# An intermediate tile of the second feed-forward stage made as two products of 256 columns

## The reference

```python
h = _ln(x) * g2 + beta2
ff = _gelu2(h @ W1 + b1) @ W2 + b2
return x + ff
```

## Time and profile before

| what | value |
|---|---|
| median of 3 runs | 2416.95 us (2416.4 to 2420.13) |
| the profiled execution, its time | 2414.24 us |
| its span | 2412.5 us |
| granted TensorE clock, mean | 0.997 |
| TensorE matmul rows, busy | 2364.6 us (98%) |
| TensorE weight loads, busy | 1891.9 us (78%) |
| DVE, ACT, POOL busy | 1349.5, 1009.7, 1017.0 us |
| matmuls | 16068 |

### The profile page before, as it was taken

One profiled execution on the slowest core, in us unless ns is written; L12 is line 12 of the kernel. 1 busy time (PEld: TensorE's weight loads), 2 busy tenths in 40 slices (PEclk: granted clock), 3 DMA queues, 4 the chain that ended last, 5 costly groups with the idle time before them and its releaser, 6 DMA issues. The chain is left out here.

```text
span 2412.5 us, 42169 instructions
## 1 busy us (share of the span) xinstructions
PE 2364.6 (98%) x16068; PEld 1891.9 (78%) x16068; DVE 1349.5 (56%) x2749; ACT 1009.7 (42%) x2057; POOL 1017.0 (42%) x829
## 2 busy tenths in 40 slices
PE   8999999999999899999999999998999999999999
PEld 6788888888887677777777777766888888888887
DVE  7354454454556777777777777778443333323322
ACT  6132232231332776767667676767311111111111
POOL 0042242341424796767677676766112202202200
PEclk9999999999999999999999999999999999999999
DMA  7110111101123466565556566564320110110110
GB/s 229 45 44 18 43 37 41 43 17 61 43 96 115 128 192 198 160 212 162 195 162 205 168 194 191 173 190 168 129 70 1 52 52 0 52 52 5 47 35 18
DMA packets 142196, 243.92 MB, mean 101 GB/s; under 512 B 14140, under 2 KB 28620, under 8 KB 142048
## 3 DMA queue, kind: packets, MB, share of 16 engines
q1 hardware_dynamic: 142048, 241.92, 31.4%
HBM read 216.69 MB, written 25.20 MB: 100 GB/s over the span
## 5 line engine op out<-in xcount | busy, mean ns | idle before, releaser
L1218 POOL TENSOR_TENSOR at_bias<-at_bias,at_mask 128x512 f32<-128x512 f32 x512 | 591.8, 1185 | 234.4 <-DMA at_bias<-in_fside_Bx16xSxS 212.3
L645 ACT ACTIVATE L_hid<-bank,L_b1c 128x512 f32<-128x512 f32 x256 | 176.6, 690 | 963.4 <-PE bank L290 958.6
L837 DVE CAST L_hh<-L_hid 128x512 fp32r<-128x512 f32 x256 | 122.5, 478 | 748.5 <-PE bank L946 715.1
L288 PE MATMUL bank<-xth,L_w1h 128*128 128x512 f32 x1024 | 402.9, 393 | 1.4 <-DVE xtl L730 1.4
L944 PE MATMUL bank<-L_w2h,L_hh 128*128 128x512 f32 x1024 | 401.1, 392 | 0.0
L289 PE MATMUL bank<-xth,L_w1l 128*128 128x512 f32 x1024 | 399.4, 390 | 0.0
L290 PE MATMUL bank<-xtl,L_w1h 128*128 128x512 f32 x1024 | 399.2, 390 | 0.0
L946 PE MATMUL bank<-L_w2l,L_hh 128*128 128x512 f32 x1024 | 398.7, 389 | 0.0
L945 PE MATMUL bank<-L_w2h,L_hl 128*128 128x512 f32 x1024 | 398.5, 389 | 0.0
L1274 ACT ACTIVATE at_bias<-at_bias,cos_sin 128x512 f32<-128x512 f32 x512 | 363.2, 713 | 9.1 <-DVE cos_sin L1412 9.1
L1412 DVE CUSTOM_DVE_ANT_0 at_bias<-bank,at_bias 128x512 f32<-128x512 f32 x512 | 331.7, 683 | 36.7 <-PE bank L1595 24.0
(11 more groups left out here) (205 smaller groups left out, 3211.4 us busy)
## 6 DMA issues: line engine op xcount, KB each, us to landing
at_bias<-in_fside_Bx16xSxS SPq DMA_DIRECT2D x256, 512.0 KB, 3.7
L_ring<-in_L_cond_w SPq DMA_DIRECT2D x32, 256.0 KB, 4.6
L_xres<-in_x SPq DMA_DIRECT2D x8, 1024.0 KB, 5.3
x_scratch<-L_xres SPq DMA_DIRECT2D x8, 1024.0 KB, 4.3
at_xres<-x_scratch SPq DMA_DIRECT2D x32, 256.0 KB, 4.3
L_xin<-x_scratch SPq DMA_DIRECT2D x8, 1024.0 KB, 5.6
L_xres<-x_scratch SPq DMA_DIRECT2D x8, 1024.0 KB, 5.5
L_xin<-in_x SPq DMA_DIRECT2D x7, 1024.0 KB, 5.3
```

Source lines behind the costliest of these rows:

```text
L288: nc_mm = pe.matmul(out, ah, bh, start=i == 0, stop=False)
L645: nc.scalar.activation(hid[m % 2][:, :], turn[m % 2][:, :], func, bias=b1c[:, m:m + 1]).then_inc(h_act, 1)
L1218: nc.gpsimd.tensor_tensor(tile, tile, mask[:, m % TT, :], ALU.add).then_inc(masked, 1)
```

## The change

For the second feed-forward stage alone, `up` calls `split_product` twice for each intermediate tile: first for columns 0 to 255 of the moving operand and of the bank, then for columns 256 to 511. Each call has its own 12 matmuls with their 12 weight loads, the same 12 weight blocks in both. The waits stay ahead of the first call, and the last matmul of the second call increments `h_mm`. The first stage and all else are as before.

```diff
             c, cut = m // TT, slice(m % TT * P, (m % TT + 1) * P)
-            split_product(pe, turn[m % 2][:, :], [(w1h[:, c, k, cut], w1l[:, c, k, cut], xth[:, k, :], xtl[:, k, :])
-                                                  for k in range(KT)]).then_inc(h_mm, 1)
+            spans = [slice(0, S)] if l0 else [slice(0, S // 2), slice(S // 2, S)]
+            for n in spans:
+                mm = split_product(pe, turn[m % 2][:, n], [(w1h[:, c, k, cut], w1l[:, c, k, cut], xth[:, k, n], xtl[:, k, n])
+                                                           for k in range(KT)])
+            mm.then_inc(h_mm, 1)
```

## The result

The changed kernel takes 2439.29 us in the median of four runs (2438.13 to 2440.27), the kernel before 2416.8 us. The ratio is 1.0089, with a 95% interval from 1.0076 to 1.0103: slower by 22.5 us, outside the 0.2% that a measurement can tell. Forecast were 2437.4 us, a range from 2416 to 2449, and slower with a chance of 0.77.

What follows compares the result with a forecast made beforehand. TensorE, never kept waiting in the second feed-forward stage, was taken as the bound. 1536 x (2 x 120.0 - 226.7 ns) = +20.5 us on the 2416.95 us median gave about 2437.4 us, range 2416 to 2449.

Steps and rivals of the forecast that it cites:

- TensorE bounds the stage: Second feed-forward stage: matmuls cover every microsecond and nobody keeps TensorE waiting, so what up matmuls lose goes into the span whole.
- One cycle a column and a fixed part: Split-product matmuls: 0.4167 ns a column plus 13.3 ns that do not shrink with the width; chance 0.62.
- p: Up product of the second feed-forward stage: pitch of one matmul of 256 columns, forecast at 120.0 ns.
- The proportional rival: Narrow up matmuls: the extra 13.3 ns shrink with the columns, change 0 to +4.6 us, 2417 to 2421; chance 0.15.
- The load is just hidden: Narrow up matmuls: a weight load holds up at most 0.11 us, less than 0.12, so nothing is charged.
- a load in part: Narrow up matmuls: load and weight swap follow each other, 123.3 ns, +30.6 us, 2447.6 us; chance 0.10.
- whole (190): Narrow up matmuls: next load only after the recorded end of the one ahead, 190 ns or more, 2652 us; chance 0.05.
- The faster rival: Narrow up matmuls escape the wide one's extra, only the load limits: 110 ns, -10.3 us, 2406.7 us; chance 0.08.
- Instructions come in time: Up product: a load and matmul each 120 ns against attention's pair each 93.5 ns; supply does not bind, nothing charged.
- The sum, +20.5 us: Second feed-forward stage: 1536 x (2 x 120.0 - 226.7 ns), the whole forecast cost of the change.
- the down matmuls stay at 0.227: Down product of the second feed-forward stage: its matmuls keep their pitch of 0.227 us beside narrow up ones.
- The reason given for the fixed part: Split-product matmuls: each of 512 columns swaps weights once, as each of 256 would, so 13.3 ns stay fixed.

## Why the prediction was right

- **TensorE bounds the stage.** Right: it is busy for all of 94 us after as before, and ACT and DVE wait longer. What the matmuls cost went into the stage whole. That no line of the waits is TensorE's was read too generously: the list from 1680 us on has some, but they are attention's last products, and one load of L288 with 0.2 us.
- **One cycle a column and a fixed part.** Right: p = 120.0 ns was forecast and is measured, and the line holds at four widths. The proportional rival (113.4 to 114.9) falls with it: at 384 columns it would have given 170 to 171 ns, not 173.3. The Trainium skill ("TensorE: Matmul & The Clock Gate", Back-to-back issue gap) would have 162.5 ns there with its 2.5 ns of fixed part, and 109.2 for a half; for this split product the trace contradicts it at every width. That section gives the rule for a single matmul and not for a stream of loads and matmuls, which the prediction did not say.
- **The load is just hidden.** Right, and the cover was as thin as said. The floor is 111.7 ns, so 120.0 clears it by 8.3; with 192 or 128 columns the matmul no longer does. The earlier trace rows could not tell the load from the transpose ahead of it, and transposes start each 109 ns in any case; that their 0.11 us came so near the floor is in part luck. The rivals of a load in part (123.3) or whole (190) fall. The faster rival needed that halves lose their fixed part; they don't. The Trainium skill's 106.7 ns for a load (same page, LDWEIGHTS) is near the floor, 5.0 ns under it.
- **Instructions come in time.** Right: four quarters take a pair each 111.7 ns, and attention's L1612 one in 32 ns.
- **The sum, +20.5 us.** One term was missing: the return from narrow to wide matmuls. It is not paid by all 128 tiles: in each of the 8 batches 14 down products come directly behind a narrow up product, and once attention's last products do. 113 x 20 ns are 2.26 us, and 20.48 + 2.26 = 22.74, the stage's growth. I had written that the down matmuls stay at 0.227; their first five don't. The trace of the kernel before had the delay. The earlier trace rows stop just short of it: behind L945 at 2317.44 the next starts are 2317.67 and 2317.91, 231 ns each in the median of the stage's 14 such places. And the stage's first matmuls, behind attention's of 128 columns (L1612), start like this:

```profile
1687.32 0.39 PE L289 MATMUL bank<-xth,L_w1l 128*128 128x512 f32 x1
1687.56 0.40 PE L290 MATMUL bank<-xtl,L_w1h 128*128 128x512 f32 x1
1687.79 0.39 PE L288 MATMUL bank<-xth,L_w1h 128*128 128x512 f32 x1
1688.02 0.40 PE L289 MATMUL bank<-xth,L_w1l 128*128 128x512 f32 x1
```

The pitches from the first of these on are 231, 236, 228, 233 and 230 ns. (A small slip beside it: 1536 x 2.5 ns are 3.8 us, not 3.9.)
- **The reason given for the fixed part** (each matmul swaps weights once) is neither shown nor refuted. It does not shrink with the load, nor does it vanish for equal weights. So the choice between a fixed and a proportional part, on which most of the 20.5 us hang, was right on a reason that stays unproved.

## What to carry to other kernels

Where one engine is busy without a gap, price a split by the pitch from start to start, not by the recorded length (the profile models where a matmul ends), and separate what goes with the columns from what each instruction pays: here 13.3 ns of 226.7, so halving the width costs 6% of the product. Two shapes of another format were enough to find the slope, and one pair of loads behind short matmuls to guess the floor. Below about 236 columns (an estimate: there columns / 2.4 + 13.3 falls under 111.7 ns; measured are 256 columns above it and 192 below) the floor takes over, and a split costs more than its 13.3 ns.

## What was not expected of the hardware

- Behind narrower matmuls, those of 512 columns in the split product take 233, 236, 228, 233 and 231 ns before they are back at 226.7: 20 ns net for each return, after 6 narrow ones of 256 columns as after 24, in either product, 3 ns after a single pair, none without a change of the moving width. Also 384 columns behind 512 start with 171 to 185 ns. What in the engine does this stays open; no run takes it apart.
- Split-product matmuls of 192 and of 128 columns, each with its load of 128 stationary columns, both start no faster than each 111.7 ns in the mean, although each load is recorded with 188 to 192 ns. The transposes, plain float32 with loads as wide, start each 109 ns.
- Half the stationary columns make a matmul of 512 moving ones no shorter (230 ns against 226.7).
- The attention stage, the same in all kernels here, took 909 to 923 us in the profiled executions. Against that, the second feed-forward stage has 742.5 us in both kernels that have the same code for it.
